# A two-layer graph attention kernel: GpSimd adds the second layer's mask, and loads, gate and scores' mask change their places

## The reference, cut to what matters

```
x = layernorm(x + Attention(x))      # 6 heads of 64, softmax(QK'/8 + where(adj, 0, -9e15)) V, then Wf
h = x @ W (12 heads of 32);  th = tanh(h)
attn[n, m] = th[n].w_src + th[m].w_dst          # per head
attn = leaky(attn, 0.2);  attn = where(adj, attn, -999);  attn = softmax(attn)
f = elu(attn @ h + b);  gate = sigmoid(x @ H_w.T + H_b)
x = layernorm(x + gate * f + (1 - gate) * x)
```

## Time and profile before

| what | us |
|---|---|
| median of 3 runs | 1215.51 (1211.43 to 1215.69) |
| profiled execution, its own time | 1212.56 |
| its span, first to last instruction | 1210.8 |
| PE busy | 1119.5 (92%) |
| DVE busy | 1029.2 (85%) |
| ACT busy | 885.1 (73%) |
| POOL busy | 550.1 (45%) |

### The profile page before, as it was taken

One profiled execution on the slowest core, in us unless ns is written; L12 is line 12 of the kernel. 1 busy time (PEld: TensorE's weight loads), 2 busy tenths in 40 slices (PEclk: granted clock), 3 DMA queues, 4 the chain that ended last, 5 costly groups with the idle time before them and its releaser, 6 DMA issues.

```text
span 1210.8 us, 25654 instructions
## 1 busy us (share of the span) xinstructions
PE 1119.5 (92%) x8364; PEld 897.3 (74%) x8428; DVE 1029.2 (85%) x2086; ACT 885.1 (73%) x3319; POOL 550.1 (45%) x717
## 2 busy tenths in 40 slices
PE   0989999999999999999999999999999999998874
PEld 0767787788778777887878778777877877786652
DVE  2527989989898998989899898989899898988886
ACT  2236878788778878877887787778787877877775
POOL 3324445445443635553454445444445454444332
PEclk9989999999999999999999999999999999998997
DMA  6401001010010101010010101002010100100000
GB/s 161 138 6 32 30 14 67 14 60 15 18 63 7 67 15 60 15 45 36 8 66 15 67 8 67 15 8 66 14 67 15 60 15 8 41 14 15 15 14 20
DMA packets 25894, 44.67 MB, mean 37 GB/s; under 512 B 2462, under 2 KB 23714, under 8 KB 25762
## 3 DMA queue, kind: packets, MB, share of 16 engines
q1 hardware_dynamic: 22368, 41.29, 9.9%
q10 hardware_dynamic: 3362, 1.73, 0.8%
q0 software_dynamic: 32, 0.00, 0.0%
HBM read 30.43 MB, written 12.58 MB: 36 GB/s over the span
## 4 chain that ended last, share of the span: by engine, by line
ACT 36%; PE 33%; DVE 16%; issue 8%; POOL 4%; ACTq 2%; POOLq 0%; DVEq 0%
ACT z L581 20%; PE ps_b L247 9%; PE ps_a L247 8%; PE ps_d L247 5%; ACT p L608 5%; DVE z L910 5%; POOL xT_lo L923 3%; PE ps_d L450 3%; ACT p1T L591 2%; DVE s L773 2%; PE ps_s L350 2%; ACT gate L657 2%; DVE p1T L757 2%; ACT ctxT_hi L646 2%; DVE s L892 2%
## 5 line engine op out<-in xcount | busy, mean ns | idle before, releaser
L581 ACT ACTIVATE z<-z,s 128x128 f32<-128x128 f32 x768 | 298.9, 403 | 0.5 <-DVE s L798 0.5
L945 POOL TENSOR_SCALAR s<-s 128x1 f32<-128x1 f32 x128 | 28.6, 224 | 339.7 <-DVE s L894 311.6
L608 ACT ACTIVATE p<-ps_s,s 128x128 f32<-128x128 f32 x384 | 135.4, 372 | 57.9 <-DVE s L773 57.8
L960 POOL TENSOR_TENSOR p<-p,s 128x768 f32<-128x768 f32 x64 | 94.2, 1472 | 147.7 <-DVE s L804 147.7
L581 ACT ACTIVATION_READ_ACCUMULATOR z<-z,s 128x1 f32 x768 | 155.5, 202 | 0.0
L450 PE MATMUL ps_d<-ident,z 128*128 128x128 f32 x768 | 120.9, 281 | 18.1 <-ACT z L581 9.1
L674 ACT ACTIVATE z<-ps_d 128x512 f32<-128x512 f32 x192 | 100.4, 595 | 42.7 <-remote 42.7
L968 POOL TENSOR_TENSOR thw<-th,w_sd 128x768 f32<-128x768 f32 x64 | 117.8, 1840 | 5.2 <-ACT th L629 5.1
L910 DVE SCALAR_TENSOR_TENSOR z<-ps_d,z 128x512 f32<-128x512 f32 x192 | 118.7, 674 | 0.0
L450 PEld LDWEIGHTS ps_d<-ident,z 128*128 128x128 f32 x768 | 91.2, 142 | 33.5 <-ACT gate L657 17.6
L599 ACT ACTIVATE x1T_hi<-ps_b 128x384 fp32r<-128x384 f32 x64 | 31.5, 492 | 100.5 <-PE ps_b L397 100.5
(11 more groups left out here) (158 smaller groups left out, 3521.3 us busy)
## 6 DMA issues: line engine op xcount, KB each, us to landing
x_cols<-in_xT_dram SPq DMA_DIRECT2D x16, 768.0 KB, 6.5
xb<-in_x_dram SPq DMA_DIRECT2D x16, 768.0 KB, 4.9
out_dram<-y SPq DMA_DIRECT2D x64, 192.0 KB, 1.8
z<-in_L_gnn_Wq_dram SPq DMA_DIRECT2D x1, 576.0 KB, 6.7
p1T<-in_L_gnn_Wk_dram SPq DMA_DIRECT2D x1, 576.0 KB, 9.0
qT<-in_L_gnn_Wv_dram SPq DMA_DIRECT2D x1, 576.0 KB, 11.5
kT<-in_L_gnn_Wf_dram SPq DMA_DIRECT2D x1, 576.0 KB, 13.8
z<-in_L_gnn_W_dram SPq DMA_DIRECT2D x1, 576.0 KB, 4.0
```

The source lines that it names most:

```text
L581: done = act.activation(z[:, a, :], z[:, a, :], ACT.Exp, bias=neg1[:, a:a + 1], accum_out=sum1[:, a:a + 1])
L608: last = act.activation(p0[:, o, i, :], ps_s[:, o, i * N:(i + 1) * N], ACT.Exp, bias=neg0[:, k:k + 1], accum_out=sum0[:, k:k + 1])
L960: pool.tensor_tensor(p0[:].rearrange("p o i n -> p (o i) n"), p0[:].rearrange("p o i n -> p (o i) n"), inv0.unsqueeze(2).broadcast_to([P, ...
```

## The change

1. The mask is now 0 or -2^53 itself. `ident_53` and `ident_100` go; the scores' mask matmuls use `ident_b`.
2. In `logits` the three mask matmuls go; the remaining matmul of each bank starts the accumulation. GpSimd adds the mask to z in SBUF, in three additions of four heads (`z_mask`), at the start of the next step; VectorE's maxima of z wait for `zm_ready` instead of `z_ready`.
3. The scores' mask matmuls are issued at the end of the step before, between `logits` and `apply_p1` (`scores_mask`).
4. ScalarE evacuates the gate before its p1T copy.
5. GpSimd's order in a step becomes: z_mask, second norm (of graph tl - 3), p0, thw, first norm (of graph ta - 1), mask quarters 1 to 3 in steps 1 to 3, xb, next xT_lo. Only quarter 0 is made at the start.
6. The seven small loads move from ScalarE's queue to SyncE's, after four weights. `small_constants` and the bias product move behind the V work of group 0.

```
@@ sync
             for n, name in enumerate(W_ORDER):
+                if n == 4:
+                    sp.dma_start(bv_col[:], bv).then_inc(S["const_in"], 16)
...
+                    sp.dma_start(hb_row, Hb.rearrange("(o d) -> o d", o=1)).then_inc(S["const_in"], 16)
                 if n >= 4:
                     sp.wait_ge(S["weight_lo"], n - 3)
@@ tensor
-            def scores(t, g, par, j):
+            def scores_mask(t):
                 if due(t):
                     pe.wait_ge(S["p0T_even"], t)
                     pe.wait_ge(S["p0T_odd"], t)
+                if t % (B // 4) == 0:
+                    pe.wait_ge(S["mask_ready"], t // (B // 4) + 1)
+                if t == 0:
+                    pe.wait_ge(S["consts_ready"], 1)
+                    pe.wait_ge(S["bf_ready"], 1)
+                for o in range(2):
+                    pe.matmul(ps_s[:, o, 0:C * N].rearrange("p (i n) -> p i n", i=C), ident_b[:],
+                              mask[:, t, :].unsqueeze(1).broadcast_to([P, C, N]), start=True, stop=False)
...
@@ logits
+                pe.wait_ge(S["rows_ready"], t + 1)
+                pe.wait_ge(S["cols_ready"], t + 1)
                 for q in range(3):
                     if due(t):
                         pe.wait_ge(S[f"p1T_{q}"], t)
-                    pe.matmul(heads, ident_100[:], m.broadcast_to([P, 4, N]), start=True, stop=False)
-                    last = pe.matmul(heads, rows_L[:, q, :], cols_R[:], start=False, stop=True)
+                    last = pe.matmul(heads, rows_L[:, q, :], cols_R[:], start=True, stop=True)
...
                     if gat:
                         logits(tl)
+                    if 0 <= ta and ta + 1 < B:
+                        scores_mask(ta + 1)
                     if tail:
                         apply_p1(tl - 1, (j + 1) % 2, gat)
@@ scalar
-                    if tail:
-                        turned_p1(tl - 1, 1)
                     if gat:
                         act.wait_ge(S["gate_made"], tl + 1)
...
+                    if tail:
+                        turned_p1(tl - 1, 1)
@@ vector
-                        dve.wait_ge(S["z_ready"], 3 * (tt + 1))
+                        dve.wait_ge(S["zm_ready"], 3 * tt + 2)
...
+                        dve.wait_ge(S["zm_ready"], 3 * (tt + 1))
                         dve.tensor_reduce(neg1[:, 8:12], z[:, 8:12, :], AX_X, ALU.max, negate=True
@@ gpsimd
+            def z_mask(t):
+                for q in range(3):
+                    pool.wait_ge(S["z_ready"], 3 * t + q + 1)
+                    pool.tensor_tensor(z[:, 4 * q:4 * q + 4, :], z[:, 4 * q:4 * q + 4, :],
+                                       mask[:, t, :].unsqueeze(1).broadcast_to([P, 4, N]), ALU.add
+                                       ).then_inc(S["zm_ready"], 1)
+            def second_norm(t):
+                pool.wait_ge(S["mv1_ready"], 2 * t + 2)
+                if t >= 2:
+                    pool.wait_ge(S[f"y_stored_{t % 2}"], 16 * (t // 2))
+                normalise(r1[:], mv1, ve1, rs1, nm1, EPS / 4, y[:, t % 2, :], "ln1_small", 3 * t, "y_ready")
...
                 for j in range(G):
+                    if tail:
+                        z_mask(tl - 1)
+                    if has_tail(n, j, 3):
+                        second_norm(tl - 3)
                     if att:
                         pool.wait_ge(S["inv0_ready"], ta + 1)
...
+                    if 0 <= ta - 1 < B:
+                        first_norm(ta - 1)
+                    if ta == 0:
+                        moved_constants()
+                    if 0 <= ta - 1 < 3:
+                        mask_quarter(ta)
+                    if qkv and j in (1, 2) and n > 0:
+                        xb_with_bias(g, par, slice(2 * j - 2, 2 * j))
                     if qkv and n + 1 < NG and j == 3:
                         x_lo(g + 1, 0)
                         x_lo(g + 1, 1)
```

More of the change, by code:

```diff
@@ L200, in _ @@
             for n, name in enumerate(W_ORDER):
+                if n == 4:
+                    sp.dma_start(bv_col[:], bv).then_inc(S["const_in"], 16)
+                    sp.dma_start(choose[:], pick_in).then_inc(S["const_in"], 16)
+                    for s, w in enumerate((w_src, w_dst)):
+                        sp.dma_start(w_sd[:, s, :], w.partition_broadcast(P)).then_inc(S["const_in"], 16)
+                    sp.dma_start(bf_in, bf.partition_broadcast(P)).then_inc(S["const_in"], 16)
+                    sp.dma_start(b1_all[:], b1.partition_broadcast(P)).then_inc(S["const_in"], 16)
+                    sp.dma_start(hb_row, Hb.rearrange("(o d) -> o d", o=1)).then_inc(S["const_in"], 16)
                 if n >= 4:
@@ L325, in bias_product, with scores @@
                 last.then_inc(S["bvf_made"], 1)
-            def scores(t, g, par, j):
+            def scores_mask(t):
                 if due(t):
                     pe.wait_ge(S["p0T_even"], t)
-                if due(t):
                     pe.wait_ge(S["p0T_odd"], t)
+                if t % (B // 4) == 0:
[6 more added lines that the diff above has]
+                              mask[:, t, :].unsqueeze(1).broadcast_to([P, C, N]), start=True, stop=False)
+            def scores(g, par, j):
                 if j == 0:
@@ L334, in scores @@
                     pe.wait_ge(S["qk_b_ready"], 3 * g)
[L335 to L338, removed]
                 for i in range(C):
@@ L476, in iteration @@
                     if att:
[L477 to L481, removed]
+                        if ta == 0:
+                            scores_mask(0)
+                        scores(g, 1 - par, j)
                     if has_tail(n, j, 2):
@@ L493, in iteration @@
                         fill_b(g, n, j)
+                    if n == 0 and j == 3:
+                        bias_product()
                     if att:
@@ L775, in iteration @@
                                           AX_X, ALU.max, negate=True).then_inc(S["neg_ready"], 1)
-                    if n == 0 and j == 3:
-                        dve.wait_ge(S["bvf_made"], 1)
-                        dve.tensor_tensor(bf_all[:], ps_s[:, 0, 0:D], bf_in, ALU.add).then_inc(S["bf_ready"], 1)
                     if gat:
@@ L844, in iteration @@
                                           ALU.add).then_inc(S["sd_ready"], 1)
-                    if n == 0 and j == 0:
-                        small_constants()
                     if qkv and j == 0:
@@ L856, in iteration @@
                         weight_parts(3 + j)
+                    if n == 0 and j == 3:
+                        small_constants()
+                        dve.wait_ge(S["bvf_made"], 1)
+                        dve.tensor_tensor(bf_all[:], ps_s[:, 0, 0:D], bf_in, ALU.add).then_inc(S["bf_ready"], 1)
                     if att:
@@ L930, in _, with mask_quarter, moved_constants, xb_with_bias @@
             pool.memset(minus_one[:], -1.0).then_inc(S["minus_one_ready"], 1)
-            pool.wait_ge(S["adj_in"], 16)
-            for s in range(4):
+            def mask_quarter(s):
                 quarter = slice(B // 4 * s, B // 4 * (s + 1))
-                pool.tensor_scalar(mask[:, quarter, :], adj_u8[:, quarter, :], 1.0, -1.0, ALU.mult, ALU.add
+                pool.wait_ge(S["adj_in"], 16)
+                pool.tensor_scalar(mask[:, quarter, :], adj_u8[:, quarter, :], 2.0 ** 53, -(2.0 ** 53), ALU.mult, ALU.add
                                    ).then_inc(S["mask_ready"], 1)
[L937 to L941, removed]
+            def moved_constants():
+                pool.wait_ge(S["hb_small"], 5)
+                pool.wait_ge(S["padding_ready"], 2)
+                pool.dma_start(hb_rows[0:3, :], hb_split[:]).then_inc(S["hb_moved"], 16)
+                pool.wait_ge(S["const_in"], 16 * 7)
+                pool.tensor_scalar(b1_all[:], b1_all[:], 1.0, None, ALU.add).then_inc(S["b1_ready"], 1)
+            def xb_with_bias(g, par, at):
+                pool.wait_ge(S["xb_in"], 16 * (g + 1))
+                if g == 0:
+                    pool.wait_ge(S["bf_ready"], 1)
+                pool.tensor_tensor(xb[:, par, at, :], xb[:, par, at, :],
+                                   bf_all[:].unsqueeze(1).broadcast_to([P, 2, D]), ALU.add
+                                   ).then_inc(S["xb_ready"], 1)
+            mask_quarter(0)
             def normalise(r, mv, ve, rs, nm, eps, out_ap, small, count, ready):
@@ L950, in normalise, with first_norm @@
                 pool.tensor_scalar(out_ap, r, nm, rs, ALU.add, ALU.mult).then_inc(S[ready], 1)
+            def z_mask(t):
[9 more added lines that the diff above has]
+                normalise(r1[:], mv1, ve1, rs1, nm1, EPS / 4, y[:, t % 2, :], "ln1_small", 3 * t, "y_ready")
+            def first_norm(t):
+                pool.wait_ge(S["mv0_ready"], 2 * t + 2)
+                if due(t - 7):
+                    pool.wait_ge(S["r1_ready"], t - 7)
+                normalise(r0[:], mv0, ve0, rs0, nm0, EPS, x1[:, t // G % 2, t % G, :], "ln0_small", 3 * t, "x1_ready")
```

(4 more changed lines are left out.)

21 lines of the change are left out of this document (2 added, 19 removed).

## The result

The changed kernel takes 1275.9 us in the median (1272.9 to 1277.84, 4 runs) against 1215.1 us of the kernel before on the same chip: 1.0505 times as long, 95% interval 1.0474 to 1.0536. Forecast were 1239 us and a range up to 1262. The direction was right, the size was not: +60.8 us by the medians, where the prediction's own sum had +26.6.

A forecast was written before the change was run, and what follows sets the result against it. VectorE, not the 98% busy TensorE, was taken to set the step. From 1212.56 us, -18.5 for the start, +46.1 for late p0 in the steady steps and -1 for the drain gave 1239 us, range 1200 to 1262.

The forecast's parts named there:

- the three matmuls: Logits mask matmuls removed from TensorE: about 0.65 us a step, taken as worth 0 because VectorE sets the step.
- The mask's move: Scores' mask matmuls issued one step earlier, before TensorE's product with p1T: nothing saved, 0.
- gate first: ScalarE evacuates the gate one p1T copy earlier: hidden in the steady state, may show in the last three steps.
- my own formula, 0.93 + 3(d - 1.20): Lateness in us of the p0T copy in j = 1 and 2 steps; d is one GpSimd mask addition, taken as 1.20.
- B: Not forecast; named in the experiments: the loss by VectorE's long 24-element cast beside GpSimd's xb.
- the start: Later small loads and constants: first projection at 11.4 instead of 29.73; taken as -18.5 us, between -20 and -13.
- The other GpSimd moves: First normalisation, xb and three mask quarters, placed after thw: 0, at most a few us in the first steps.
- T: Start of VectorE's first z instruction (L910), the last thing it does in a step; times in a step count from it.
- the 0.93 us of lateness: p0T copy at T+8.77 instead of T+7.84 in j = 1 and 2 steps, carried by VectorE to the next z.
- A: Named in the experiments: the loss by the late p0; the prediction's steady sum for it was +46.1 us.
- the drain: Last three steps, without scores, where the earlier gate may show: booked as -1 us, between -3 and +3.
- the rival of the clock: TensorE idles before turning p0, so its granted clock falls in some 25 steps, 1 us each: 1264 us; chance 0.10.

The follow-up runs named there:

- experiment 4: Kernel before without the second layer's mask: three logits mask matmuls left out, nothing in their place (output not the reference's); 1214.2 us, ratio 1.0018.
- 6: Changed kernel with the mask matmuls back, no additions to z, and xb directly behind thw, ahead of the first normalisation; 1196.6 us, ratio 0.9872.
- 7: Kernel before with only the changed start: seven small loads on SyncE's queue, small constants and bias product behind group 0's V products; 1194.9 us, ratio 0.9872.
- experiment 1: Changed kernel with one more wait: GpSimd adds the output bias to xb only after VectorE has split s and d; 1232.2 us, ratio 1.0168.
- experiment 3: Kernel before with one more wait: GpSimd starts xb in j = 1 and 2 only after VectorE has made ctxT_lo; 1252.4 us, ratio 1.0323.
- experiment 5: Changed kernel with xb behind the split, second layer's normalisation behind thw instead of ahead of p0, and r1 existing twice; 1201.5 us, ratio 0.9916.
- e_start_again: Second run of the kernel before with only the changed start (small loads on SyncE's queue, later constants and bias product); 1194.2 us, ratio 0.9852.

## Why the prediction was wrong, step by step

**Right.** VectorE and not TensorE sets the step; the three matmuls are worth 0 (experiment 4: ratio 1.0018). The mask's move and gate first are worth 0 (6 against 7). The additions make p0 late and so lengthen j = 0, 1 and 2 but not j = 3. Their length was put at 1.20 us and is 1.14 from start to start; my own formula, 0.93 + 3(d - 1.20), gives 0.75 for that, measured 0.77, and for j = 0 1.08, measured 1.07. For the steps 5 to 59 these come to 28 x 0.77 + 13 x 1.03 = 35 us, 42.4 forecast; with B taken away (experiment 1) the j = 1 step loses 0.70 instead of 0.77. The Trainium skill's 2.6 cycles an element (GPSIMD Engine Reference, section 3.1) make an estimate of 1.11 us before dispatch, 0.03 below the 1.14; my 1.20, from a row of 1839 ns whose second operand is twice as wide, is 0.06 above it. Both are near.

**Roughly right.** The first projection came at 11.28 (11.4 forecast), the first scores at 38.67 instead of 37: TensorE waited 2.57 us for bf_all, of which I had 1.3. At the third step the gain was 17.4 us, at the fourth 15: in the step between, a mask quarter and xb fell on the split, as these lines show, so the start was worth 15 us there and not 18.5.

```profile
77.37 0.90 DVE L865 CAST sd<-sd 128x24 bf16<-128x24 f32 x1
78.31 1.75 DVE L867 TENSOR_TENSOR sd_rest<-sd 128x24 f32<-128x24 f32 x1
...
76.34 1.90 POOL L936 TENSOR_SCALAR mask<-x 128x2048 bf16<-128x2048 uint8 x1
...
78.21 1.81 POOL L952 TENSOR_TENSOR xb<-xb,bf_all 128x768 f32<-128x768 f32 x1
```

**Wrong: the step that failed** is the sentence "The other GpSimd moves (first normalisation and xb, three mask quarters in steps 1 to 3) ... 0, and at most a few us in the first steps". It asked who waits for xb, by semaphores, and found nobody. It did not ask what VectorE executes meanwhile. Its own figures held the meeting: it put xb from T+11.7 to T+13.5, and the cast, 10.82 us behind T before, with the 0.93 us of lateness at T+11.75. Measured, the moves put xb from T+8.50, right behind thw, to T+11.42, onto the cast at T+11.58. VectorE works without a gap from there to the next z, so it passes the 1.57 us on to the end of the step, less the 0.17 us that it used to wait for TensorE before cols_R; TensorE and ScalarE, which wait for sd3, are late with it. Step lengths give 2.13 - 0.77 = 1.36 us in j = 1 and 2, 28 x 1.36 = 38 us; experiment 1 takes it away (41 us), experiment 3 makes it alone (39 us). With these 38 us the forecast would have been 1277, which is nearer to the measured time than the rest of the sum deserves: A came 7 us smaller than forecast, the start 3.5 us smaller, and the last steps dearer, as said below.

The row that could have told it was in the trace before: while GpSimd made the mask (until 28.39 us), VectorE's wq_lo took 3.04 us, and wk_lo, of the same size, right behind 1.34. The prediction took wq_lo at 1.35 and did not ask about the difference.

```profile
19.50 8.89 POOL L935 TENSOR_SCALAR mask<-x 128x2048 bf16<-128x2048 uint8 x4 [18.01 <-DMA x<-in_adj_dram]
...
26.55 3.04 DVE L704 TENSOR_TENSOR wq_lo<-z,wq_hi 128x1152 fp32r<-128x1152 f32 x1
29.51 1.34 DVE L704 TENSOR_TENSOR wk_lo<-p1T,wk_hi 128x1152 fp32r<-128x1152 f32 x1
```

From step 60 to the end, another 8 us were lost, of which 3 are A (3.7 forecast); the other 5 stand against the -1 that was booked for the drain. The granted clock fell there more than before (0.75 from 1180 to 1200 us and 0.82 from there on; before, 1.00 from 1140 to 1180 us and 0.85 to 1200); how much of the 5 is the clock's was not tested and stays open. Between 200 and 1050 us it stayed at 1.00, so the rival of the clock did not come true there.

## What to carry to other kernels

When an instruction moves on GpSimd, write beside it what VectorE runs at its new place, not only who waits for it: in these traces instructions with two SBUF operands, and most casts from SBUF to SBUF, stood still until GpSimd's instruction ended, however small they were. Work put into an engine's idle time is cheap only as long as what others wait for still starts on time: 3.4 us of additions and 2.0 of normalisation ahead of p0 cost 31 us more than the same additions with the normalisation moved behind p0. And an engine that is 98% busy may have nothing to give: read which engine never waits.

## What the runs showed of the hardware

VectorE's 24-element cast takes 0.17 us alone and up to 1.74 us beside GpSimd's 128x768 addition, ending within 0.05 us of that addition's end; a subtraction of two SBUF operands took 1.75 instead of 0.18. The reduction of thw (one operand, 0.94 us, beside xb in the kernel before) and a copy out of PSUM (0.69 us, beside xb in experiment 1) keep their length. Not every cast is held either. In e_start_again the cast of rows_L lies beside GpSimd's xT_lo and takes 0.55 us, as it does alone in the kernel before, while the next cast, cols_R, takes 1.49 us instead of 0.42:

```profile
36.06 1.80 POOL L923 TENSOR_TENSOR xT_lo<-x_cols,xT_hi 128x768 fp32r<-128x768 f32 x1 [1.42 <-ACT xT_hi L549]
...
36.07 0.55 DVE L715 CAST rows_L<-choose 64x384 bf16<-64x384 f32 x1
36.65 1.49 DVE L717 CAST cols_R<-choose 64x512 bf16<-64x512 f32 x1
```

Alone, the cast that is held is the quicker one an element (0.42 us for 512 elements a partition against 0.55 for 384); no run varies this by itself.

The Trainium skill names the contention (GPSIMD Engine Reference, sections 1 and 8): GpSimd shares its SBUF interfaces with VectorE and contends with VectorE's two-port modes and with two SBUF inputs. The traces agree for the two inputs; that the held casts run in such a mode and rows_L's does not would fit, but no run here shows it. The size is in the traces: the small instruction does not run slower in proportion, it waits for the whole of the large one when it starts just behind it. GpSimd's own instruction is hardly longer for it (1.86 against 1.84 us). Beside GpSimd's short instructions the price is small: in the j = 3 step of experiment 5 that ends at 589.37, where the normalisation's instructions lie beside the split, its dearest instruction (the second cast, at 583.82) took 0.46 us instead of 0.18.
